# An audio block with routed experts on one core: later layer norm for the second half, roots by Newton steps, weights by quarters

## The chip, the core and the metric

One core of a Trainium2 chip runs the whole program. The core has five engines with queues of their own: TensorE (matmuls and transposes; PE), VectorE (DVE), ScalarE (ACT), GpSimd (POOL) and SyncE (SP, which issues transfers here). They wait for one another by semaphores. The metric is device time in microseconds, the median of several executions. Before the change it is 421.42 us (three runs, 420.96 to 422.04).

## The reference

The input x has 64 sequences of 125 steps with 128 features.

```
h   = QRNN(x)                 # window 3, tanh and sigmoid gates, scan over 123 steps
h   = h + gelu(longconv(LN(h)) + h0 * LN(h))
u   = LN(h)                   # layer norm over 128 features, the "second" one
p   = u @ gate.T              # 16 experts; top 2 of each token, softmax of the two as weights
s_e = sum over tokens that chose e of silu(u @ w1_e.T)
y_e = (s_e / count_e) @ w2_e.T
out = h + w_1 * y_(expert 1) + w_2 * y_(expert 2)
```

An expert gives one mean vector, so each token's u goes through w1 of its two experts, and only the sums are kept.

## The kernel before, in words

H holds h as 123 steps (partitions) x 64 sequences x 128. Up to 158 us the recurrent cell and the long convolution fill it. Then comes routing, in four quarters of 16 sequences, and then 138 expert tiles of 128 tokens.

The second layer norm has its statistics on VectorE (`bn`, one bn_stats per sequence, L1504; `moments2`, L1512 to L1520, makes variance `ve2`), its root on GpSimd (a power of -0.5, L594), `shift` on VectorE (L1525) and the rows themselves on ScalarE (`norm2`, L1186) and GpSimd (L597), 8 of 16 each in quarters 0 to 2 and all 16 on ScalarE in quarter 3. `write_table(g)` on SP (L504) stores a quarter of the normalized rows to a table in HBM, when both engines are done with it.

The router doesn't need normalized rows: `x2_transposes` (L714) and `logits` (L705) work on H, sixteen sets of four sequences, through a ring of two PSUM banks (`PR`) that ScalarE's `copy_x2T` (L1195) reads. The same ring takes the transposes of w1 (`w1_transposes` L697, `copy_w1T` L1123) and the products `matches` (L785), which ScalarE turns into one-hots (`low_onehots`, L1223). For each quarter VectorE does `top2` (L1554 to L1564, twelve dependent steps, with other work put between them by `between`), TensorE `ranks` (L738 to L757, waits for the mask), VectorE `counts` (L1568) and `places` (L1574 to L1591), TensorE `bit_transposes` (L777), ScalarE `copy_bits` (L1216), TensorE `matches` and `picks` (L768), ScalarE `copy_V` (L1210), TensorE `pick_transposes` (L793), VectorE `placed` (L1609, L1611). `codes` (L895) and `index_list` (L1693, L1695) then make a list of token rows by expert.

There are two lists. The first serves tiles 0 to 41, from quarters 0 and 1; the second the rest. `idx_ready` counts them. GpSimd then issues one indirect transfer (L614, a gather) for each tile, in order, from the table into a tile row. The first waits for list 1 and for quarters 0 and 1 of the table. Tile rows 0 to 59 are the rows of XN, in which the normalized sequences lay; so gather 32 waits until `write_table(2)` and `write_table(3)` have landed (`table_out[1]`), and gather 42 for list 2. `paces` holds a few more gathers behind steps of the routing:

```
paces = {8: (count_mm, 3), 12: (bits_mm, 3), 16: (pick_mm, 3), 20: (count_mm, 4), 23: (bits_mm, 4),
         27: (pick_mm, 4), 32: (code_mm, 2)}
```

A tile goes through TensorE (three transposes at a time, L905; one product with w1 of its expert, L935), ScalarE (silu, L1265) and VectorE (addition into `esum`, L1712). TensorE may be five tiles ahead of the additions. The first product waits for all of w1T; the first addition waits for four transfers that clear `esum`, each behind a set of w1 transposes (`clear`, L510, on SP's queue in the order written). Between the additions of tiles 15 to 18 VectorE makes the weights of the picks, all quarters at once (two products L1788, a sum L1790); TensorE transposes them at tiles 23 and 26 (`RT_AT`, L1025), ScalarE and VectorE split them in two parts (L1278, L1797). Behind the last tile come the means, w2 and the output.

On every engine instructions run in the order in which the code lists them, so a waiting instruction holds all that are behind it on that engine.

## Time and profile before

| what | us |
|---|---|
| median of the runs | 421.42 |
| the profiled execution | 420.74 |
| its span, first to last instruction | 419.0 |
| routing, from the last addition of the convolution to the first expert product | 158.6 to 234.6 |
| gathers, first to last issue | 199.74 to 373.66 |
| expert products and the last one's end | 234.56 to 381.97 |

Busy shares of the span are PE 91%, DVE 74%, ACT 52% and POOL 49%. A busy TensorE isn't TensorE at its peak, since pipelined matmuls are counted whole; what is read here is who waits for whom in each stretch. A row of a timeline gives start and duration in us, the engine, the line, the operation and, in brackets, how long the engine idled before it and what ended that. Rows that follow one another with the same form are merged (x16: sixteen). The granted clock (PEclk) is 1.00 at full speed, 2.4 GHz, and 0.50 at 1.2 GHz.

### The profile page before, as it was taken

The numbers are of one execution on the slowest core, as the hardware profiler recorded it, in microseconds if no ns is written. First come the engines' busy times: TensorE is split into PE (matmuls) and PEld (weight loads), VectorE is DVE, ScalarE is ACT, GpSimd is POOL, SyncE is SP. The second block draws the span as 40 slices with busy tenths as digits, with TensorE's granted clock in tenths as the row PEclk, the third lists the DMA queues.
The fourth block names the chain that finished last, engine by engine and source line by source line (L and its number), as shares of the span: only waits on it lengthen the run. The fifth ranks groups of instructions, "written<-read, shape, count | busy, mean of one in ns | idle before, by whom it ended". The sixth has DMA issues, their size and how long they took to land.

```text
span 419.0 us, 7310 instructions
## 1 busy us (share of the span) xinstructions
PE 379.5 (91%) x1929; PEld 261.9 (63%) x1930; DVE 310.8 (74%) x827; ACT 217.6 (52%) x423; POOL 206.0 (49%) x231
## 2 busy tenths in 40 slices
PE   7999999999978998977785998899999998999892
PEld 7888888888868998864553543444444443334471
DVE  3399887878796879999877278577777675557892
ACT  2433555555551334667747864576676664565310
POOL 2011211111164004999777777777777777752600
PEclk9999999999989999996866998999999999999997
DMA  6400843433132058330475621111771111110068
GB/s 163 133 2 13 218 132 89 128 91 96 48 98 77 22 158 245 99 96 2 145 243 195 209 59 44 50 52 56 257 251 53 50 56 50 53 49 0 1 162 225
DMA packets 53020, 43.68 MB, mean 104 GB/s; under 512 B 20686, under 2 KB 45980, under 8 KB 52732
## 3 DMA queue, kind: packets, MB, share of 16 engines
q1 hardware_dynamic: 44276, 32.09, 26.2%
q0 software_dynamic: 4416, 9.05, 7.3%
q10 hardware_dynamic: 4296, 2.15, 1.9%
q8 instruction: 15, 0.25, 0.3%
q14 instruction: 17, 0.14, 0.1%
HBM read 34.86 MB, written 8.42 MB: 103 GB/s over the span
## 4 chain that ended last, share of the span: by engine, by line
PE 55%; DVE 17%; POOL 16%; issue 6%; ACT 4%; DMA 1%; DVEq 0%; ACTq 0%; POOLq 0%
PE P L662 22%; PE P L935 11%; PE P L867 7%; POOL BIG L614 7%; POOL arena L614 5%; DVE H L1828 3%; DVE BIG L1712 3%; PE P L697 2%; PE P L1062 2%; PE P L655 2%; PE P L905 2%; PE P L688 2%; POOL XN L597 2%; DVE arena L1504 1%; POOL arena L594 1%
## 5 line engine op out<-in xcount | busy, mean ns | idle before, releaser
L935 PE MATMUL P<-w1T,arena 128*128 x276 | 129.0, 601 | 3.2 <-DVE BIG L1712 2.6
L1712 DVE TENSOR_TENSOR BIG<-BIG,P 128x512 f32 x138 | 94.9, 688 | 49.9 <-ACT P L1265 34.3
L935 PEld LDWEIGHTS P<-w1T,arena 128*128 128x128 f32 x276 | 48.5, 191 | 50.2 <-issue 49.5
L1265 ACT ACTIVATE P<-P 128x512 f32<-128x512 f32 x138 | 72.8, 580 | 1.6 <-PE P L935 1.5
L614 POOL DMA_INDIRECT XN<-table,arena x60 | 59.5, 991 | 19.1 <-issue 19.1
L557 POOL TENSOR_TENSOR rs<-ve,mhalf 123x4 f32<-123x4 f32 x16 | 17.5, 1096 | 101.8 <-DVE ve L1356 101.8
L1103 ACT ACTIVATE arena<-P 128x492 f32<-128x492 f32 x48 | 27.9, 583 | 50.3 <-PE P L662 50.3
L1254 ACT COPY arena<-P 128x384 f32<-128x384 f32 (+1 forms) x48 | 22.4, 467 | 53.4 <-PE P L935 53.3
L614 POOL DMA_INDIRECT arena<-table,arena x42 | 39.7, 944 | 12.8 <-issue 12.2
L662 PE MATMUL P<-xh,wh 128*128 128x498 f32 x144 | 42.4, 403 | 0.0
L662 PE MATMUL P<-xh,wl 128*128 128x498 f32 x144 | 40.5, 390 | 0.0
L662 PE MATMUL P<-xl,wh 128*128 128x498 f32 x144 | 40.4, 389 | 0.0
L614 POOL DMA_INDIRECT BIG<-table,arena x36 | 34.0, 944 | 11.0 <-issue 10.7
L662 PEld LDWEIGHTS P<-xl,wh 128*128 128x128 f32 x144 | 27.3, 190 | 5.6
L662 PEld LDWEIGHTS P<-xh,wl 128*128 128x128 f32 x144 | 27.1, 188 | 5.4
L867 PE MATMUL P<-XN,BIG 123*123 123x112 f32 (+1 forms) x256 | 27.7, 271 | 1.1 <-DVE XN L1401 1.1
L662 PEld LDWEIGHTS P<-xh,wh 128*128 128x128 f32 x144 | 26.2, 192 | 4.1
L867 PEld LDWEIGHTS P<-XN,BIG 123*123 123x123 f32 x256 | 27.6, 188 | 1.3 <-DVE XN L1401 1.3
L594 POOL TENSOR_TENSOR arena<-arena,mhalf 123x16 f32<-123x16 f32 x4 | 11.7, 2923 | 31.6 <-DVE arena L1520 31.6
L1359 DVE SCALAR_TENSOR_TENSOR arena<-arena 128x492 f32<-128x492 f32 x16 | 10.7, 669 | 17.2 <-ACT arena L1103 17.2
L597 POOL TENSOR_SCALAR XN<-H,arena 123x128 f32<-123x128 f32 x24 | 23.3, 985 | 0.3
L1499 DVE TENSOR_TENSOR H<-H,arena 123x512 f32<-123x512 f32 x16 | 20.2, 1279 | 3.7 <-ACT arena L1177 3.7
(242 smaller groups left out, 617.4 us busy)
## 6 DMA issues: line engine op xcount, KB each, us to landing
arena<-kpad SPq DMA_DIRECT2D x16, 492.0 KB, 4.0
XN<-in_L_ffn_w SPq DMA_DIRECT2D x1, 4096.0 KB, 17.0
arena<-in_x SPq DMA_DIRECT2D x16, 224.0 KB
table<-XN SPq DMA_DIRECT2D x4, 896.0 KB
BIG<-table SPq DMA_DIRECT2D x1, 2048.0 KB, 9.3
out<-H SPq DMA_DIRECT2D x8, 224.0 KB
out<-H ACTq DMA_DIRECT2D x8, 224.0 KB
BIG<-table SPq DMA_DIRECT2D x1, 1024.0 KB, 4.8
```

Of the source, the lines that this page charges most:

```text
L557: nc.gpsimd.tensor_tensor(rs1[0:T, k], ve1[0:T, k], mhalf[0:T, 0:CB], ALU.pow).then_inc(rstd1, 1)
L594: nc.gpsimd.tensor_tensor(rs2[0:T, qb], ve2[0:T, qb], mhalf[0:T], ALU.pow).then_inc(rstd2, 1)
L597: a = nc.gpsimd.tensor_scalar(XN[0:T, b], H[0:T, b], mm2[0:T, 0, b:b + 1], rs2[0:T, b:b + 1], ALU.subtract, ALU.mult)
L614: pool.indirect_dma_start(out=row_of(n), out_offset=None, in_=table[0:(QA * QB + 1) * TROW, :] if n < NA else table[:, :], in_offset=bass. ...
L662: mm = nc.tensor.matmul(PG[g][:, 0:NV], wpart[:, w, g * D:(g + 1) * D], xpart[:, k, w:w + NV], start=(place == 0 and w == 0), stop=(place ...
L867: mm = nc.tensor.matmul(PG[g % 3][0:T, j * B:j * B + n], hank[0:T, c // HP % HRES, c % HP], XF[0:T, c * B:c * B + n], start=True, stop=True)
L935: mm = nc.tensor.matmul(bank[:, :], stat, w1T[:, bass.ds(e * FF, FF)], start=True, stop=True)
L1103: nc.scalar.activation(dst[:, k].rearrange("p (b t) -> p b t", b=CB), src, func).then_inc(gate_act, 1)
L1254: nc.scalar.copy(GTs[:, bank, 0:count * SLOT], PT[:, 0:count * SLOT]).then_inc(GT_ready, 1)
L1265: nc.scalar.activation(bank[:, :], bank[:, :], ACT.Silu).then_inc(silu_done, 1)
L1499: v.tensor_tensor(hv, hv, gl[0:T, g % 2], ALU.add).then_inc(H_added, 1)
L1712: v.tensor_tensor(at, at, bank[:, :], ALU.add).then_inc(esum_step, 1)
```

## The change

- **The second half's layer norm** (quarters 2 and 3) moves behind the first list: its statistics, moments and shifts leave the places between the steps of top2(0) and top2(1) and go between and behind those of top2(2), top2(3) and the new steps.
- **The roots** of quarters 2 and 3 are made on VectorE by `rstd_by_steps`: an integer first guess and three Newton steps, eleven dependent operations on 123x16, with other work between them. GpSimd makes those of quarters 0 and 1 alone, both ahead of its norm rows.
- **The norm rows** of quarters 2 and 3 are all ScalarE's (`NORM_POOL`), at new places of its queue; four rows of quarter 1 go behind copy_V(0).
- **x2 and w1 sets**: thirteen sets of x2 come ahead of the first list, three behind it; no w1 set stands ahead of it (two did).
- **stay_warm**: matmuls of 256 or 512 columns into a bank that isn't read, on TensorE ahead of its waits in the routing.
- **The weights** of the picks are made by quarters, one operation of 256 columns behind each of the additions 14 to 25; the transposes come at tiles 23 and 32.
- clear(11, 0, 4) goes ahead of write_table(2) on SP.

The diff, without the lines around each place:

```diff
...
-NORM_POOL = (8, 8, 8, 0)
+NORM_POOL = (8, 8, 0, 0)
+X2_FIRST = 13
...
-        at_ring = 2 * NHB
-        for part, q in ((range(0, 2), 0), ((), 1), (range(2, 10), 2), (range(10, 12), 3)):
+        X2_AT = list(range(X2_FIRST))
+        at_ring = X2_FIRST
+        for part, q in (((), 0), ((), 1), (range(0, 10), 2), (range(10, 12), 3)):
+            if q == 2:
+                X2_AT += range(at_ring, at_ring + 2 * NHB - X2_FIRST)
+                at_ring += 2 * NHB - X2_FIRST
...
-        RT_AT = (23, 26)
+        R_AT = 14
+        RT_AT = (23, 32)
...
+            clear(11, 0, 4)
-            clear(11, 0, 4)
...
-            def norms(g):
+            def rstd_of(g):
+            def norms(g):
...
-            norms(0)
+            rstd_of(0)
+            rstd_of(1)
+            norms(0)
-            norms(2)
-            norms(3)
...
+            def stay_warm(n, wide=False):
+                place = P[1][:, :] if wide else P[3][:, 256:512]
+                cols = oneb[:].unsqueeze(1).to_broadcast([128, 4 if wide else 2, 128])
+                for _ in range(n):
+                    nc.tensor.matmul(place, oneb[:], cols, start=True, stop=True)
...
-                pe.wait_ge(ring_read, n + 1)
+                pe.wait_ge(ring_read, X2_AT[n] + 1)
...
-                if n >= 2:
-                    pe.wait_ge(ring_read, n - 1)
+                at = X2_AT[n]
+                if at >= 2:
+                    pe.wait_ge(ring_read, at - 1)
-                    mm = nc.tensor.transpose(PR[n % 2][:, q * T:(q + 1) * T], H[0:T, 4 * n + q], ident[0:T, 0:T])
+                    mm = nc.tensor.transpose(PR[at % 2][:, q * T:(q + 1) * T], H[0:T, 4 * n + q], ident[0:T, 0:T])
...
+                stay_warm((0, 4, 2, 1)[q], q >= 2)
...
+                    if n == ON_ACT - OG:
+                        stay_warm(3 if q < 2 else 1, q >= 2)
...
+                stay_warm((5, 6, 8, 4)[q], q >= 2)
+                stay_warm((4, 3, 1, 5)[q], q >= 2)
+                    if a == 2 and q == 0:
+                        tile_base(1)
+                    if a == 2 and q != 2:
+                        stay_warm(3 if q == 3 else 5, q == 3)
...
+                stay_warm(2 if q >= 2 else 4, q >= 2)
...
+                if nth == 2:
+                    stay_warm(4, True)
...
+                    if c >= chunks - 2:
+                        stay_warm((2 if c == chunks - 2 else 1) * (2 if nth == 1 else 1), nth == 2)
...
-            for n in range(2 * NHB):
+            for n in range(X2_FIRST):
-                if n == 11:
+                if n == 10:
-                if n == 15:
+                if n == 12:
-            logits(2 * NHB - 1)
+            logits(X2_FIRST - 1)
-            for m in range(0, 2):
-                w1_transposes(m)
-            tile_base(1)
...
-            for m in range(2, 8):
+            for n in range(X2_FIRST, 2 * NHB):
+                x2_transposes(n)
+                if n > X2_FIRST:
+                    logits(n - 1)
+            logits(2 * NHB - 1)
+            for m in range(0, 5):
-            for m in range(8, 10):
+            for m in range(5, 10):
...
-                    pe.wait_ge(R_ready, 1)
+                    pe.wait_ge(R_ready, 2 * (RT_AT.index(n) + 1))
...
-                act.wait_ge(ring_mm, n + 1)
+                act.wait_ge(ring_mm, X2_AT[n] + 1)
-                nc.scalar.copy(x2T[:, n % 2].rearrange("p b t -> p (b t)"), PR[n % 2][:, 0:4 * T]).then_inc(ring_read, 1)
+                nc.scalar.copy(x2T[:, n % 2].rearrange("p b t -> p (b t)"), PR[X2_AT[n] % 2][:, 0:4 * T]).then_inc(ring_read, 1)
...
-            for n in range(12, 16):
-                if n == 14:
-                    code_OH(0)
-                for b in NORM_ACT[1][2 * (n - 12):2 * (n - 11)]:
-                    norm2(b)
-                copy_x2T(n)
+            copy_x2T(12)
+            code_OH(0)
+            for b in NORM_ACT[1][:4]:
+                norm2(b)
-            for m in range(0, 2):
-                copy_w1T(m)
+            for b in NORM_ACT[1][4:]:
+                norm2(b)
-            for b in NORM_ACT[2]:
-                norm2(b)
-            for m in range(2, 8):
+            for n in range(X2_FIRST, 2 * NHB):
+                copy_x2T(n)
+            for m in range(0, 5):
...
-            for b in NORM_ACT[3][:6]:
+            code_OH(2)
+            for m in range(5, 10):
+                copy_w1T(m)
+            for b in NORM_ACT[2][:3]:
-            code_OH(2)
-            for m in range(8, 10):
-                copy_w1T(m)
+            for b in NORM_ACT[2][3:5]:
+                norm2(b)
+            code_OH(3)
+            for b in NORM_ACT[2][5:8]:
+                norm2(b)
-            code_OH(3)
+            for b in NORM_ACT[2][8:10]:
+                norm2(b)
-            for b in NORM_ACT[3][6:]:
+            for b in NORM_ACT[2][10:]:
+            for b in NORM_ACT[3]:
+                norm2(b)
...
-            shift(0)
...
-            top2(0, more_stats(2))
-            for b in range(2 * QB + (4 * 11 + 2) // 3, 3 * QB):
-                bn(b)
-            counts(0)
-            moments2(2)
-            shift(1)
+            def shifts(i):
+                if i in (2, 8):
+                    shift(i // 8)
+            top2(0, shifts)
+            def rstd_by_steps(g, between):
+                qb = slice(g * QB, (g + 1) * QB)
+                var, y = ve2[0:T, qb], rs2[0:T, qb]
+                square, half = mm2[0:T, 1, qb], mm2[0:T, 2, qb].bitcast(I32)
+                def then(ins, i):
+                    rs[0] += 1
+                    ins.then_inc(route_step, 1)
+                    between(i)
+                    dve.wait_ge(route_step, rs[0])
+                dve.wait_ge(ve2_ready, g + 1)
+                then(v.tensor_scalar(half, var.bitcast(I32), 1, None, ALU.arith_shift_right), 0)
+                then(v.tensor_scalar(y.bitcast(I32), half, -1.0, float(0x5F3759DF), ALU.mult, ALU.add), 1)
+                for k in range(3):
+                    then(v.tensor_tensor(square, y, y, ALU.mult), 3 * k + 2)
+                    then(v.scalar_tensor_tensor(out=square, in0=square, scalar=-0.5, in1=var, op0=ALU.mult,
+                                                op1=ALU.mult), 3 * k + 3)
+                    a = v.scalar_tensor_tensor(out=y, in0=square, scalar=1.5, in1=y, op0=ALU.add, op1=ALU.mult)
+                    if k == 2:
+                        a.then_inc(rstd2, 1)
+                    else:
+                        then(a, 3 * k + 4)
...
-            top2(1, more_stats(3))
-            for b in range(3 * QB + (4 * 11 + 2) // 3, 4 * QB):
-                bn(b)
+            def count_first(i):
+                if i == 2:
+                    counts(0)
+            top2(1, count_first)
-            moments2(3)
-            shift(2)
...
-            shift(3)
-            top2(2, nothing)
+            top2(2, more_stats(2))
+            for b in range(2 * QB + (4 * 11 + 2) // 3, 3 * QB):
+                bn(b)
+            moments2(2)
+            def stats_of_last(i):
+                bn(3 * QB + i)
+            rstd_by_steps(2, stats_of_last)
+            shift(2)
...
+            for b in range(3 * QB + 10, 4 * QB):
+                bn(b)
+            moments2(3)
-            placed(2)
-            low_onehots(3, 0)
+            def places_of_last(i):
+                if i == 2:
+                    placed(2)
+                if i == 5:
+                    low_onehots(3, 0)
+            rstd_by_steps(3, places_of_last)
+            shift(3)
...
-            for n in range(16):
+            def weight(k, q):
+                w = wgt[0:T, 1 + k, q * QB:(q + 1) * QB].unsqueeze(2).to_broadcast([T, QB, E])
+                rs[0] += 1
+                v.tensor_tensor((L, Ltmp)[k][0:T, q * QB:(q + 1) * QB], OH[0:T, q, k], w,
+                                ALU.mult).then_inc(route_step, 1)
+            def weights(n):
+                q, part = (n - R_AT) // 3, (n - R_AT) % 3
+                if part < 2:
+                    weight(part, q)
+                else:
+                    dve.wait_ge(route_step, rs[0])
+                    both = L[0:T, q * QB:(q + 1) * QB]
+                    v.tensor_tensor(both, both, Ltmp[0:T, q * QB:(q + 1) * QB], ALU.add).then_inc(R_ready, 1)
+            for n in range(R_AT):
-            by_quarter = [a[0:T].rearrange("p (q b) e -> p q b e", q=NQ) for a in (L, Ltmp)]
-            for k, dst in enumerate(by_quarter):
-                w = wgt[0:T, 1 + k].rearrange("p (q b) -> p q b", q=NQ).unsqueeze(3).to_broadcast([T, NQ, QB, E])
-                step(v.tensor_tensor(dst, OH[0:T, :, k], w, ALU.mult))
-                add_tile(16 + k)
-            v.tensor_tensor(L[0:T], L[0:T], Ltmp[0:T], ALU.add).then_inc(R_ready, 1)
-            for n in range(18, UNROLLED):
+            for n in range(R_AT, UNROLLED):
+                if n < R_AT + 3 * NQ:
+                    weights(n)
```

## Rows read from the trace of the kernel before

**Rows 1.** GpSimd's timeline (start us, us, engine, line, operation), first list to end

```profile
199.74 1.23 POOL L614 DMA_INDIRECT XN<-table,arena  x1 [1.17 <-issue]
...
240.74 0.94 POOL L614 DMA_INDIRECT XN<-table,arena  x1 [0.30 <-issue]
...
254.47 1.75 POOL L614 DMA_INDIRECT XN<-table,arena  x1 [0.30 <-issue]
...
259.02 1.94 POOL L614 DMA_INDIRECT XN<-table,arena  x1 [0.30 <-issue]
...
373.66 0.94 POOL L614 DMA_INDIRECT arena<-table,arena  x1 [0.30 <-issue]
```

**Rows 2.** TensorE's timeline, expert matmuls (L935)

```profile
234.56 2.84 PE L935 MATMUL P<-w1T,arena 128*128 x6 [0.17 <-issue]
...
267.97 2.74 PE L935 MATMUL P<-w1T,arena 128*128 x6
...
343.50 2.74 PE L935 MATMUL P<-w1T,arena 128*128 x6
...
375.78 1.02 PE L935 MATMUL P<-w1T,arena 128*128 x2
```

**Rows 3.** VectorE's timeline, ahead of the first list and the step behind it

```profile
167.12 0.41 DVE L1554 TENSOR_REDUCE arena<-P 123x16 f32<-123x256 f32 x1
...
173.51 0.27 DVE L1564 TENSOR_TENSOR BIG<-BIG 123x256 bf16<-123x256 bf16 x1
...
182.85 0.16 DVE L1568 CAST arena<-P 128x2 bf16<-128x2 f32 x1
...
183.80 0.68 DVE L1574 TENSOR_REDUCE arena<-P 123x32 f32<-123x512 f32 x1
...
198.63 0.25 DVE L1695 TENSOR_SCALAR arena<-arena,route_sb 128x42 int32<-128x42 int32 x1
...
199.04 0.40 DVE L1554 TENSOR_REDUCE arena<-P 123x16 f32<-123x256 f32 x1
```

**Rows 4.** VectorE's timeline, its idle times behind the first list

```profile
204.91 0.16 DVE L1568 CAST arena<-P 128x2 bf16<-128x2 f32 x1 [0.82 <-PE P L738]
...
215.16 0.16 DVE L1568 CAST arena<-P 128x2 bf16<-128x2 f32 x1 [1.11 <-PE P L738]
...
216.76 0.69 DVE L1574 TENSOR_REDUCE arena<-P 123x32 f32<-123x512 f32 x1 [1.30 <-PE P L749]
...
223.66 0.18 DVE L1765 TENSOR_SCALAR arena<-P 128x16 f32<-128x16 f32 x1 [2.78 <-PE P L879]
```

**Rows 5.** TensorE's timeline, transposes (L714) and 512-column matmuls (L729)

```profile
178.62 0.58 PE L714 MATMUL P<-ident,H 123*128 123x123 f32 x4
...
179.90 0.58 PE L714 MATMUL P<-ident,H 123*128 123x123 f32 x4
...
180.32 0.60 PE L729 MATMUL P<-samef,arena 128*123 128x512 bf16 x2
...
198.20 1.94 PE L729 MATMUL P<-samef,arena 128*123 128x512 bf16 x4
```

**Rows 6.** ScalarE's timeline, copy_bits, Relus and norm rows

```profile
191.21 0.26 ACT L1216 CAST arena<-P 128x123 bf16<-128x123 f32 x1 [0.22 <-PE P L777]
...
221.11 2.72 ACT L1223 ACTIVATE BIG<-P,below 123x512 bf16<-123x512 f32 x4 [0.57 <-PE P L785]
...
223.73 3.94 ACT L1186 ACTIVATE XN<-H,arena 123x128 f32<-123x128 f32 x10
```

**Rows 7.** DMA issues by size: median us from issue to landing

```profile
BIG<-table SPq DMA_DIRECT2D x1, 1024.0 KB, 4.8
...
BIG<-table SPq DMA_DIRECT2D x2, 512.0 KB, 6.1
```

**Rows 8.** VectorE's timeline, the sum of the weights

```profile
258.93 1.22 DVE L1790 TENSOR_TENSOR arena<-arena 123x1024 f32<-123x1024 f32 x1
```

**Rows 9.** stretches: us, busy (x) of PE, PEld, DVE, ACT, POOL, PEclk, DMA

```profile
192.00:194.00 2.00, 1.23 (x4) 0.35 (x2) 2.00 (x2) 1.56 (x3) 2.00 (x2) 0.50 0.00 0
```

## The prediction

> **What bounds the kernel now.** I read the chain of waits first, then the timelines of GpSimd, VectorE, TensorE and ScalarE from 158 us on. The chain gives the expert matmuls the stretch from 234 to 292 us and GpSimd's gathers the rest; the GpSimd timeline says more. Its 138 gathers run from 199.74 to 373.66 us [rows 1], all 1.25 us apart but for a few that last longer, and none of them idles more than the fixed 0.30 us ahead of it: the stream is one unbroken chain, and its start decides its end. The experts run at 75.53/26 = 2.905 us per three tiles between 267.97 and 343.50 us; at that pace tile 132 would start at 343.50 + 9 x 2.905 = 369.65 us, and it starts at 375.78 [rows 2]. So the expert stream has 6.1 us of slack, and the gathers bound the end. Everything behind the last gather is unchanged.
>
> The first gather follows the first list (VectorE's row at 198.63, done at 198.88 [rows 3]) by 0.86 us. VectorE is busy from 158 us to there almost without a gap, which is why work taken out of it ahead of the list should count.
>
> The profiled execution took 420.74 us, 0.68 us below the median of the runs, 421.42. The sum is made on the former and 0.68 added.
>
> **Ahead of the first list.** Thirty-two bn_stats, two moments2 and four shifts leave; two shifts return inside top2(0). top2(0) with its fill takes 167.12 to 173.51 and 0.27 for its last operation; a bare one takes 199.04 to 204.09 [rows 3, 4], 5.05. Without shift(0) it starts at 166.93, so the mask of quarter 0 is there at 166.93 + 5.05 = 172.0, that of quarter 1 near 177.0. The moments between counts(1), 182.85, and places(0), 183.80, go too: 0.87 us without the count's own 0.08, in four dependent levels, 0.22 a level [rows 3].
>
> TensorE is then late. shift(0) comes 1 us later, ScalarE's first norm2 and the copy behind it with it, and ranks(0) starts near 172.25, ends near 174.1. Up to ranks(1) stand two steps of transposes and logits (1.28 each, 178.62 to 179.90), one more set of logits (0.9), counts_behind (0.43 for two 512-column matmuls, 180.32 and what follows) and four 256-column fillers (0.43 by the same row): 4.35 us, so ranks(1) at 178.45 [rows 5]. counts(1) and places(0) follow at 178.8, against 183.80: 5.0 us gained there.
>
> It is not all kept. Five fillers stand ahead of bit_transposes(0) and end 0.55 us past the moment at which the bits are there, while the two w1 sets ahead of it are gone (0.4 us of ScalarE's copies): copy_V(0), which ended at 190.99 (0.22 of idle time ahead of 191.21 [rows 6]), ends 4.85 earlier, 186.15. ScalarE now has four norm rows (3.94/10 = 0.394 each, 1.6 us [rows 6]) between it and copy_bits(1), which so runs at 187.75, against 191.21. From there to the list it was 7.7 us, through matches, picks, copy_V(1), pick_transposes, placed(1) and codes; TensorE's part of it ran at half clock [rows 9], which I count 0.4 us shorter: **first list at 195.0, 3.9 us earlier**. Bounds: 2.8 (no clock gained, the fillers in full) and 5.0 (VectorE's own path). The wait for ScalarE's rows holds only this chain; VectorE, which would be ready for placed(1) 1 us sooner, stands idle. The table's first half, written once ScalarE's last row of quarter 1 is done (187.75), is down before that.
>
> Were nothing else late, the gathers would start and end 3.9 us earlier.
>
> **Behind the first list.** A gather has to wait there. Gather 32 overwrites row 32, which write_table(3) reads, and so waits for table_out[1]. Before, gather 32 ran at 240.74 [rows 1] with that write long down: the last norm row ended at 227.67 (223.73 + 3.94 [rows 6]). The same gather would now want to run at 236.85. I follow when ScalarE ends its last row now.
>
> VectorE: from the first list to total_mm(2) took 198.88 to 223.66, 24.8 us, of which 0.82, 1.11, 1.30 and 2.78 us are idle [rows 4]. Added: 15 bn_stats inside top2(2) and one behind (6.39 + 0.27 against 5.05, and 0.2: 1.9), moments2(2) 0.9, rstd_by_steps(2) with ten bn_stats (0.1 + 0.2 each, and a last one: 3.2 with its shift), six bn_stats 1.2, moments2(3) 0.9, rstd_by_steps(3) 2.3 (eleven levels of 0.22, less what placed(2) and low_onehots(3, 0) cover, plus its shift): 10.4 us. The idle time takes 4.9 of it: ranks(2) is ready near 203.1 (counts_behind, three sets of x2 and logits, 4.2 us with their copies, five w1 sets at the 0.6 us of a copy, two wide fillers, from 194.3 on), which leaves 0.4 idle, and total_mm(2) leaves 0.7. So this point moves from 223.66 to 195.0 + 24.8 + 5.5 = 225.3: the 3.9 us are spent and 1.6 more.
>
> TensorE and ScalarE: places(3) starts at 195.0 + 17.9 (198.88 to 216.76) + 8.1 added - 2.8 absorbed = 218.2. ranks(3) ends near 218.4; pick_transposes(2) 0.9, two w1 sets 1.0 and four wide fillers 0.85 (0.21 each) put bit_transposes(3) at 221.15, behind its bits; copy_bits to 221.7; two norm rows to 222.5; the four Relus of quarter 3's matches, started at 222.9, 2.6 us as before [rows 6], to 225.5; six rows of quarter 2, 2.4, to 227.9, by when picks(3) are done; copy_V(3) 0.35; and then all sixteen rows of quarter 3, 6.3 us, which stand behind copy_V(3) in the queue and need shift(3) besides (near 224.5): **last row at 234.55, 6.9 us later than before**.
>
> write_table(3) then needs, by the nearest rows, 4.8 us (1 MB) to 6.1 us (512 KB) from issue to landing [rows 7]; I take 5.2, near the one of its size. With 0.1 to issue and 0.4 to wake GpSimd, **gather 32 runs at 240.25**, 3.4 us after it would have and 0.5 us before its old time. The other paces (count_mm, bits_mm, pick_mm, code_mm) come at most 0.3 us from binding and earlier than this one; code_mm(2), near 238.3, is inside it.
>
> **Behind that.** Three 1.22 us operations of VectorE made the weights. Beside two of them a gather took 1.75 and 1.94 us in place of 0.94, 1.8 us in all; the one at 259.02 began just after VectorE's at 258.93 and ended 0.9 us after it [rows 1, 8]. Now twelve of about 0.33 us stand there. A gather that meets one at a random point waits half of it: 12 x (0.33/1.25) x 0.17 = 0.5 us. Gain 1.3 us; bounds 1.8 (none met) and -1.5 (ten gathers, each met for a whole one, 3.3).
> The Trainium skill, "SBUF — State Buffer", section "SBUF: two separate sides", says that a VectorE operation with two SBUF inputs and a GpSimd operation that reads SBUF exclude each other for the whole instruction. The rows agree on the blocking. By that rule, with a loss that goes with the locked time (12 x 0.33 = 4.0 us against 3.7), nothing would be regained here.
>
> The expert stream: w1T is complete behind ScalarE's last norm row and four copies, so tile 0 starts near 238.2 (234.56 before [rows 2]). The last clears of esum now queue on SP behind write_table(3); with 6.1 us each [rows 7] VectorE's first addition, and with it tile 6, comes some 4.4 us later. Against its pace from tile 0 the stream lost 267.97 - (234.56 + 9 x 2.905) = 7.3 us up to tile 27, mostly to the weights; now at most VectorE's twelve added operations stand there, 4.0 us. So it moves by 4.4 - 7.3 + 4.0 = 1.1 us at the worst and has 6.1 of slack: it stays hidden, and costs one for one past 4.3 us (6.1 less the gathers' gain).
>
> **Sum.** -0.5 (gather 32) - 1.3 (gathers less blocked) = -1.8: 420.74 - 1.8 + 0.68 = **419.6 us**.
>
> **Rivals.**
> 1. Full gain: ScalarE's last row ends by 230.7, no wait at gather 32, -3.9 - 1.3: 416.2. For it: ScalarE idles often behind 199 us, and TensorE's lower clock in the old second half may give back more than I took. Against it: sixteen rows in one piece. 14%.
> 2. No change: the first list gains only the lower bound, 2.8, everything behind shifts by 1.1 and half of the blocking gain fails (0.6): -0.1, 421.3. Here belongs the case by the rule above: -0.5 alone, 420.9. 25%.
> 3. Slower: the fillers keep no clock and stand on the path. Before, the clock was 0.50 of full speed (1.2 GHz) at 192 to 194 us while TensorE was idle for four tenths of the time [rows 9], and four 512-column matmuls took 1.94 us at 198.20 against 0.60 for two at 180.32 [rows 5]. At that level the wide ones cost 0.49 each; the four ahead of bit_transposes(3), the five ahead of matches(3) and slower w1 sets put the Relus 4.2 us later, and with them the last row, the write and gather 32: +3.7 - 1.3 = +2.4, 423.8. It is slower than before from 1.8 us of such delay on. For it: the chip falls to that level in these very gaps. Against it: the fillers close them. 14%.
> My forecast holds the rest, 47%, with 418.2 to 420.9 as its own range (landing 4.8 to 6.1, blocking 0 to 2).
>
> Faster or slower counts from 0.3% (1.26 us), about what a measurement of this kernel can tell. Faster: rival 1 and four fifths of the forecast, 0.53; slower: rival 3 and a little, 0.15; the same: 0.32. The range 416.3 to 423.0 leaves out some of rivals 1 and 3, 18% together.
>
> **What would show it.** Right: first gather near 195.9 us; a gap of 2 to 5 us on GpSimd ahead of gather 32, released by a DMA; ScalarE's last norm row near 234.5; no gather above 1.3 us beside the weights; no idle time on TensorE at tiles 23 to 32. Wrong: no gap at gather 32 (rival 1), a first gather behind 197 us, a clock near 0.5 behind the first list (rival 3), or tiles behind 120 that never wait for a gather (the expert stream then bounds).

## The result, and the profile after

The changed kernel takes 419.42 us (median of 7, 418.02 to 419.67) beside 421.58 (420.79 to 422.74) for the kernel before: ratio 0.9941, 95% interval 0.9922 to 0.9960, a gain of 0.6%. Over all 26 of its runs here it lies between 417.27 and 420.08. Its profiled execution took 419.67 us with a span of 417.9. That is 1.07 below the profile of before, while the medians stand 2.16 apart: the old profile lies 0.84 below 421.58, and the new one 0.25 above its own median.

GpSimd's timeline answers to [rows 1]: the first and the last gather, those that something other than issue held, and those over 1.0 us beside the weights.

```profile
194.81 1.23 POOL L622 DMA_INDIRECT XN<-table,arena  x1 [9.52 <-DVE arena L1756]
...
211.60 0.94 POOL L622 DMA_INDIRECT XN<-table,arena  x1 [1.69 <-PE P L797]
...
217.86 0.94 POOL L622 DMA_INDIRECT XN<-table,arena  x1 [0.79 <-PE P L787]
...
241.44 0.94 POOL L622 DMA_INDIRECT XN<-table,arena  x1 [3.36 <-DMA table<-XN]
...
260.15 1.09 POOL L622 DMA_INDIRECT XN<-table,arena  x1 [0.30 <-issue]
...
264.04 1.15 POOL L622 DMA_INDIRECT XN<-table,arena  x1 [0.30 <-issue]
...
269.24 1.16 POOL L622 DMA_INDIRECT XN<-table,arena  x1 [0.30 <-issue]
...
373.08 0.94 POOL L622 DMA_INDIRECT arena<-table,arena  x1 [0.30 <-issue]
```

The stream starts 4.93 us earlier than in [rows 1] and is broken at gather 32, which waits for the table's write: 241.44 in place of 240.74. So the lead of 4.93 is a lag of 0.70 there. Of these 5.63 us the wait takes 3.06 (3.36 less the 0.30 that stands ahead of every gather), the paces at gathers 12 and 16 take 1.39 and 0.49, and 0.7 goes to gathers that last longer than before. From gather 32 on the gathers take 131.64 us in place of 132.92, and the last is 0.58 ahead of the old one.

VectorE's timeline, for [rows 3 and 4]: the convolution's last addition, counts(1) (which waits for TensorE's ranks(1)), places(0), the first list's last operation, and the one that waits for total_mm(2).

```profile
157.47 1.24 DVE L1537 TENSOR_TENSOR H<-H,arena 123x512 f32<-123x512 f32 x1 [0.45 <-ACT arena L1209]
...
178.87 0.16 DVE L1606 CAST arena<-P 128x2 bf16<-128x2 f32 x1 [1.59 <-PE P L755]
178.94 0.68 DVE L1612 TENSOR_REDUCE arena<-P 123x32 f32<-123x512 f32 x1
...
194.26 0.25 DVE L1756 TENSOR_SCALAR arena<-arena,route_sb 128x42 int32<-128x42 int32 x1
...
226.26 0.18 DVE L1844 TENSOR_SCALAR arena<-P 128x16 f32<-128x16 f32 x1 [0.37 <-PE P L905]
```

ScalarE's timeline, for [rows 6]: the four norm rows, copy_bits(1), quarter 3's Relus, six rows of quarter 2, and all sixteen of quarter 3.

```profile
186.15 1.65 ACT L1218 ACTIVATE XN<-H,arena 123x128 f32<-123x128 f32 x4
187.70 0.25 ACT L1248 CAST arena<-P 128x123 bf16<-128x123 f32 x1
...
224.00 2.47 ACT L1255 ACTIVATE BIG<-P,below 123x512 bf16<-123x512 f32 x4 [0.46 <-PE P L810]
226.36 2.40 ACT L1218 ACTIVATE XN<-H,arena 123x128 f32<-123x128 f32 x6
228.84 0.37 ACT L1242 COPY arena<-P 128x256 f32<-128x256 f32 x1
229.11 6.27 ACT L1218 ACTIVATE XN<-H,arena 123x128 f32<-123x128 f32 x16
```

The last row ends at 229.11 + 6.27 = 235.38, and gather 32 runs 6.06 us later.

TensorE, for [rows 2]: ranks(1), a w1 set behind ScalarE's rows, tile 6, the first transposes of the weights, the row that stood at 343.50, the first wait for a gather, and tile 132.

```profile
178.63 0.19 PE L755 MATMUL P<-oneb,BIG 123*128 123x1 bf16 x2
...
235.99 1.94 PE L712 MATMUL P<-ident,BIG 128*128 128x128 f32 x8 [5.01 <-ACT w1T L1155]
...
247.48 2.90 PE L965 MATMUL P<-w1T,arena 128*128 x6 [0.77 <-DVE BIG L1773]
...
265.47 0.64 PE L1057 MATMUL P<-ident,arena 123*128 123x123 f32 x4 [0.57 <-DVE arena L1874]
...
345.56 2.74 PE L965 MATMUL P<-w1T,arena 128*128 x6
...
360.70 0.54 PE L935 MATMUL P<-ident,BIG 128*128 128x128 f32 x3 [0.56 <-DMA BIG<-table,arena]
...
375.20 1.02 PE L965 MATMUL P<-w1T,arena 128*128 x2
```

Its stretches, for [rows 9] (PEclk is the number behind POOL's):

```profile
192.00:194.00 2.00, 1.75 (x18) 1.06 (x18) 1.12 (x4) 0.06 (x1) 0.00 (x0) 1.00 0.26 69
...
212.00:220.00 8.00, 7.79 (x61) 3.80 (x60) 6.32 (x23) 5.55 (x11) 5.99 (x6) 0.57 0.32 114
```

The clock is full (2.4 GHz) at 192 to 194 us, where it had been half. In 212 to 220 it falls towards 1.2 GHz, as it did before the change (0.58 there), behind 1.35 us in which TensorE idled (209.65 to 211.01) for quarter 2's bits. That idle time alone isn't the reason: weights_whole, below, has the same 1.35 us there and a clock of 1.00 behind it.

### The profile page after: what moved, and what is told of

Its sections match the earlier page's. It is cut to its first block, busy times and chain, and to the rows that moved or that the text cites. A ratio compares the mean times of both kernels' runs of the same rounds, so it can differ in the third digit from the quotient of the medians.

```text
span 417.9 us, 7515 instructions
## 1 busy us (share of the span) xinstructions
PE 386.5 (92%) x2018; PEld 266.3 (64%) x2019; DVE 314.8 (75%) x858; ACT 220.5 (53%) x431; POOL 191.6 (46%) x221
## 4 chain that ended last, share of the span: by engine, by line
PE 67%; DVE 18%; ACT 6%; issue 3%; DMA 2%; POOL 1%; DVEq 1%; SPq 0%; ACTq 0%; POOLq 0%
PE P L965 23%; PE P L670 19%; PE P L893 7%; PE P L935 3%; DVE H L1919 3%; DVE BIG L1773 2%; DVE arena L1542 2%; ACT XN L1218 2%; DMA BIG<-table 2%; PE P L1094 2%; PE P L663 2%; PE P L695 2%; PE P L720 2%; PE P L703 1%; DVE arena L1403 1%
## 5 line engine op out<-in xcount | busy, mean ns | idle before, releaser
L965 PE MATMUL P<-w1T,arena 128*128 x276 | 127.4, 596 | 1.4 <-DVE BIG L1773 1.0
L1209 ACT ACTIVATE arena<-P 123x512 f32<-123x512 f32 x16 | 9.6, 598 | 21.9 <-PE P L893 20.5
L600 POOL TENSOR_TENSOR arena<-arena,mhalf 123x16 f32<-123x16 f32 x2 | 5.8, 2914 | 32.3 <-DVE arena L1558 32.3
```

Of the source, the lines that this page charges most:

```text
L965: mm = nc.tensor.matmul(bank[:, :], stat, w1T[:, bass.ds(e * FF, FF)], start=True, stop=True)
```

## The experiments

Ratios are to the kernel before on the same chip (medians 421.19, 422.17 and 421.01 in the three groups). A "profile" of an experiment is one execution.

**after_again, after_third**: the changed kernel itself, beside the first and the third group.

> The changed kernel once more, for the spread and a second trace. Theory (the gather stream bounds the end; gather 32 waits for write_table(3)): the first gather near 194.8 us, gather 32 at 240.5 to 242 behind a wait of about 3 us, the time 0.9922 to 0.996 of before. Rival (the gain of the median comes from somewhere the first trace does not show): gather 32 or the last gather at another place than 241.4 and 373.1 by over 1 us.

> The changed kernel once more, beside the three kernels below. 419.0 to 419.7 us, ratio 0.993 to 0.996; gather 32 waits 3 to 3.5 us for the table's write where the clock falls in 212 to 220 us, 1 to 1.5 us where it doesn't (as in weights_whole, whose program is the same up to there).

419.33 us (12 runs), 0.9946 (0.9929 to 0.9964), and 419.47 (7 runs), 0.9947 (0.9926 to 0.9967). Gather 32 waits 3.44 and 3.32 us in their profiles and runs at 241.35 and 241.21; the clock is 0.57 in 212 to 220 in both. The effect of the change is there each time.

**gate_split**: gather 32 waits for quarter 2's rows alone.

```
table_out: 2 semaphores -> 3, g // QA -> max(g - 1, 0)
before gather 32: - wait table_out[1] for both quarters   + for quarter 2's
before gather 42: + wait table_out[2] (quarter 3)
paces: - 32: (code_mm, 2)
```

> Gather 32 waits for write_table(2) alone (its rows are of quarter 2), gather 42 for write_table(3); code_mm(2) no longer holds gather 32. Theory: no wait at gather 32, it runs at 238.4 instead of 241.4 us, every later gather 3.0 us earlier; the expert stream has 354.28 + 6 x 2.905 = 371.7 against 375.2 us, 3.5 us of slack, so the time falls by 2.5 to 3.1 us below the changed kernel, to about 416.4 us. Rival (the expert stream, which starts 6.2 us later than before, bounds the end by now): gather 32 earlier all the same, the time within 1 us of the changed kernel.

417.94 us, 0.9929 (0.9903 to 0.9954): 1.4 us by the medians, half of what was expected, and the interval overlaps after_again's. The trace says it more clearly: the wait is gone from its GpSimd timeline, though in its profile the first gather came at 195.54:

```profile
195.54 1.23 POOL L622 DMA_INDIRECT XN<-table,arena  x1 [10.79 <-DVE arena L1757]
...
239.58 0.94 POOL L622 DMA_INDIRECT XN<-table,arena  x1 [0.30 <-issue]
...
370.74 0.94 POOL L622 DMA_INDIRECT arena<-table,arena  x1 [0.30 <-issue]
```

The gate (the one wait that holds the whole stream) did hold the gathers: the last of them is 2.34 us earlier than in the changed kernel, and from the first to the last they take 175.20 us in place of 178.27. The expert stream then waits for a gather once only, 0.24 us at 369.63: it is then close to bounding the end itself.

**half_rows**: eight of quarter 3's sixteen rows are not normalized. **half_both**: besides, five of the last six rows of quarter 2.

```
- for b in NORM_ACT[3]:           + for b in NORM_ACT[3][8:]:
- for b in NORM_ACT[2][10:]:      + for b in NORM_ACT[2][15:]:     (half_both)
```

> Left out: the normalizing of eight of the sixteen rows of quarter 3. ScalarE's last row ends 3.15 us earlier, and w1T and the first expert tile come as much earlier. Theory: gather 32 again at 238.4 us (it would run there without a wait), the time 2.7 to 3.3 us below the changed kernel, as with the wait split. Rival (the expert stream bounds): here it starts earlier too, so this one gains and the split wait does not.

> half_rows, and of the last six rows of quarter 2 all but one left out too (thirteen rows of the 32 in the second half are not normalized). Theory (half_rows gained only 1.0 us at gather 32 because the write of quarter 2's rows is issued behind their last one, at 228.7 us, and the last quarter's write queues behind it in the DMA queue): quarter 2's write is issued 1.5 to 2 us earlier, gather 32 runs before 238.7 us in place of 240.37, with a wait below 1 us, and the time is 1 to 1.7 us below half_rows', near 417.3 us. Rival (the clears of esum that share the DMA engines set the landing): gather 32 stays near 240, the time within 0.4 us of half_rows'.

half_rows: 418.82 us, 0.9943 (0.9923 to 0.9963). The expectation failed: the last row ends 3.2 us earlier, gather 32 runs 1.07 earlier. The DMA view of 228 to 246 us shows where the rest went (40 slices, busy tenths of the 16 DMA engines). First the changed kernel:

```profile
DMA  0222999999998714005899999999958999956206
```

and half_rows:

```profile
DMA  0405999999989999999999689969996753402204
```

In the changed kernel quarter 2's write is done before quarter 3's begins (the slices near zero). In half_rows the second follows on the first's heels, the engines have no gap for some twelve microseconds, and gather 32 waits to 240.37. Of the 3.2 us that ScalarE gave back 2.1 were lost there: from the last row to gather 32 it is 8.20 us in place of 6.06.

half_both: 418.46 us, 0.9933 (0.9913 to 0.9953), where near 417.3 was expected. Quarter 2's write is issued at 226.51 in place of 228.65 and gather 32 doesn't wait, but its profile's first gather came at 196.29, so it ran at 240.33 for that reason. The time lies 0.4 us below half_rows', on another chip. Whether quarter 2's write or the clears of esum, which share the DMA engines, held half_rows' gather isn't told apart.

**no_fill**: no stay_warm matmuls.

> The changed kernel without any filler matmul. Theory (the fillers hold the clock and cost a little in the path): the clock falls to 0.5 from about 188 us to the end of the first list; the first list 0 to 0.8 us later, ScalarE's last norm row and gather 32 0 to 1 us later, time +0 to +1.2 us against the changed kernel. Rival (the fillers are only in the way): first list 0.5 us earlier, last norm row 0.5 to 1.5 us earlier, time 0.5 to 1.5 us lower.

420.35 us (420.09 to 421.03, 11 runs), 0.9982 (0.9968 to 0.9996): 1.0 us above the changed kernel beside it, clear of its interval. So the fillers make 1.0 of the 1.9 us by which the changed kernel is faster there. The clock by stretches, and the steps to the first gather and gather 32:

```profile
184.00:192.00 8.00, 5.19 (x63) 3.10 (x60) 6.87 (x26) 4.97 (x11) 0.43 (x1) 0.50 0.47 126
...
212.00:220.00 8.00, 7.76 (x57) 3.68 (x58) 6.64 (x24) 5.44 (x12) 5.71 (x6) 0.50 0.34 120
```

```profile
156.97 1.24 DVE L1537 TENSOR_TENSOR H<-H,arena 123x512 f32<-123x512 f32 x1 [0.45 <-ACT arena L1209]
...
186.33 0.25 ACT L1248 CAST arena<-P 128x123 bf16<-128x123 f32 x1
...
193.73 0.25 DVE L1756 TENSOR_SCALAR arena<-arena,route_sb 128x42 int32<-128x42 int32 x1
...
194.28 1.23 POOL L622 DMA_INDIRECT XN<-table,arena  x1 [9.85 <-DVE arena L1756]
...
241.88 0.94 POOL L622 DMA_INDIRECT XN<-table,arena  x1 [3.55 <-DMA table<-XN]
```

Its first gather comes half a microsecond ahead of the changed kernel's, but that lead stands at the convolution's last addition already (156.97 for 157.47), ahead of the first filler; from there to the first gather the two take the same time. The fillers put copy_bits(1) 1.37 us later (187.70 for 186.33), 0.87 more than that lead, and the full clock gives it back: from there to the end of the list it is 6.81 us with them and 7.65 without. Behind the list they gain: without them gather 32 runs 0.44 us later, 0.94 counted from the last addition.

**fill_more**: fourteen fillers in place of eight ahead of bit_transposes(2).

```
- stay_warm((5, 6, 8, 4)[q], q >= 2)     + stay_warm((5, 6, 14, 4)[q], q >= 2)
```

> The changed kernel with fourteen in place of eight filler matmuls ahead of the transposes of quarter 2's bits, so that TensorE is not idle from 209.65 to 211.01 us, ahead of the stretch 212 to 220 us in which the granted clock falls to about 0.57. Theory (the fall of the clock there makes the second half 1 to 2 us later in most executions and not in some, which is why the changed kernel's times spread over 417.3 to 420.0 us): clock 1.00 in 212 to 220, ScalarE's last row near 234.4 in place of 235.4, gather 32 near 240.4, the time 418.3 to 418.8 us with a smaller spread. Rival (that stretch waits for VectorE's bits and places, not for TensorE): clock up, last row and time unchanged, 419.2 to 419.6 us.

418.18 us (417.31 to 418.56, 5 runs), 0.9909 (0.9884 to 0.9934). The stretch and the gathers:

```profile
212.00:220.00 8.00, 7.20 (x75) 4.41 (x74) 7.74 (x33) 6.20 (x13) 6.17 (x7) 1.00 0.33 110
```

```profile
194.83 1.23 POOL L622 DMA_INDIRECT XN<-table,arena  x1 [9.49 <-DVE arena L1756]
...
239.65 0.95 POOL L622 DMA_INDIRECT XN<-table,arena  x1 [1.05 <-DMA table<-XN]
...
371.13 0.95 POOL L622 DMA_INDIRECT arena<-table,arena  x1 [0.30 <-issue]
```

The six fillers fill 1.3 us of idle time. The clock stays full and gather 32 runs 1.79 us earlier than in the changed kernel, more than expected. That the fillers did it isn't shown: the next run, on the same chip, has the clock at 1.00 and gather 32 at 239.50 without them, and the changed kernel itself didn't run there. The ratio is 0.0037 lower than after_again's, from another chip, and the intervals overlap by a sliver.

**weights_whole**: the weights as before the change.

```
- weight(part, q) behind additions 14 to 25   + three whole operations behind additions 15 to 17
RT_AT: (23, 32) -> (23, 26)
```

> The changed kernel with the picks' weights made as before the change: three whole operations of VectorE behind additions 15 to 17, both transposes behind tiles 23 and 26; all else as changed. Theory (twelve short operations block the gathers less than three long ones, 0.58 against 1.8 us, and the expert stream, which has only 3.5 us of slack left, then loses some 4 us more at tiles 23 to 27 than now): last gather near 374.3 in place of 373.1, two gathers of 1.7 to 1.9 us, and the end 1.2 to 2.0 us later than the changed kernel's, 420.6 to 421.3 us beside its 419.4. Rival (the rule by which the loss goes with the locked time, 4.0 against 3.7 us): no later than the changed kernel, 419.0 to 419.7 us.

419.76 us (418.78 to 422.35, 9 runs), 0.9957 (0.9930 to 0.9983), where 420.6 to 421.3 was expected: the time is not told apart from the changed kernel's. The clock, TensorE's idle time ahead of that stretch and the gathers are:

```profile
212.00:220.00 8.00, 7.20 (x74) 4.38 (x75) 7.71 (x33) 6.40 (x13) 6.17 (x7) 1.00 0.30 101
```

```profile
210.85 0.32 PE L797 MATMUL P<-ident,arena 123*128 123x123 f32 x1 [1.35 <-DVE arena L1626]
```

```profile
239.50 0.94 POOL L622 DMA_INDIRECT XN<-table,arena  x1 [1.12 <-DMA table<-XN]
...
259.47 1.99 POOL L622 DMA_INDIRECT XN<-table,arena  x1 [0.30 <-issue]
...
264.26 1.94 POOL L622 DMA_INDIRECT XN<-table,arena  x1 [0.30 <-issue]
...
372.64 0.94 POOL L622 DMA_INDIRECT arena<-table,arena  x1 [0.30 <-issue]
```

From gather 32 to the last they take 133.14 us, 1.50 more than the changed kernel's 131.64, as the first theory has it. In this execution the clock was 1.00 in 212 to 220 with the code up to there unchanged, gather 32 ran at 239.50, and the loss doesn't show in its time; whether it was so in the other eight isn't known.

**paces_off, split_w1first, split_w1first_nopace, best**: the six paces at gathers 8 to 27 (in paces_off all seven) taken out; w1's last four copies ahead of ScalarE's sixteen rows and the last clears ahead of the last write, with gate_split; both; and both with fill_more's fillers.

```
paces_off, ..._nopace, best:  paces = {}
split_w1first, ..._nopace, best:  gate_split, and
+ for m in range(12, E): copy_w1T(m)      (moved ahead of NORM_ACT[3])
+ clear(13, 4, 6); clear(15, 6, 8)        (moved ahead of write_table(3))
best: fill_more's line too
```

> The changed kernel without the seven paces of GpSimd's gathers 8 to 32, its wait for the table's write kept. Theory (gather 32's wait for the write sets the second half, and covers the 1.88 us that the paces take at gathers 12 and 16): gather 31 ends 1.9 us earlier, gather 32 waits 1.9 us longer and runs when it did, and the time is within 0.4 us of the changed kernel's. Rival (the paces keep gathers from blocking VectorE, as their places suggest: without them VectorE's steps come later and the write with them): gather 32 0.5 us or more later, 0.5 to 1 us slower. Second rival (the paces cost 1.9 us whatever waits behind): 1 us or more faster.

> The table's write in three semaphores as in gate_split, and besides ScalarE's copies of the last four w1 sets ahead of its sixteen rows of quarter 3, and the last two clears of esum ahead of the last part of the table on SP. Theory (with gather 32 free, the expert stream is within a microsecond of the end, since its w1 sets stand behind the sixteen rows and its first addition behind the clears): tile 0 starts 4 to 5 us earlier than in gate_split, the expert stream never bounds, no wait for w1 sets at half clock; the time is gate_split's or up to 0.5 us below, 417.3 to 418.0 us, and tile 132 regains 3 us or more of slack. Rival (the quarter's rows come 1.5 us later and gather 42 then waits for them, or the clears and the write share the DMA engines): 0.5 to 1.5 us slower than gate_split.

> split_w1first without the six paces that make GpSimd wait, at gathers 8 to 27, for TensorE's signals. Theory (the paces cost what the idle times at gathers 12 and 16 show, 1.39 + 0.49 = 1.9 us in the changed kernel, and nothing takes their place while the expert stream has slack): gathers end 1 to 1.9 us earlier than in split_w1first, 415.5 to 417.0 us. Rival (without the paces the gathers block VectorE's steps of the second half or are blocked by them, or the last rows' write then holds gather 42): within 0.4 us of split_w1first.

> split_w1first_nopace with fill_more's fourteen fillers. Theory (both together: the gathers are an unbroken chain from the first list on, so the fillers' gain in the second half now lies off the path): within 0.5 us of split_w1first_nopace, 415.4 to 416.4 us, 3 to 4 us below the changed kernel beside it, with nothing left on GpSimd but gathers that last longer beside VectorE. Rival (a clock that falls in 212 to 220 us in some executions delays the index list of the second half, code_mm and the last rows enough to hold gather 32 or 42): 0.5 to 1 us faster still by its median, and a smaller spread.

paces_off: 418.67 us (417.38 to 419.98), 0.9941 (0.9920 to 0.9963), beside 419.47, 0.9947: no difference that can be measured. Gather 32 still waits for the table's write, so its wait covers the paces:

```profile
240.36 0.94 POOL L622 DMA_INDIRECT XN<-table,arena  x1 [2.36 <-DMA table<-XN]
```

The wait didn't grow by 1.9 us, as the theory had it, but is 1.0 shorter. The clock was 1.00 in 212 to 220 in that profile, and the write came 1.1 us earlier; the gathers up to 31 last 1.4 us longer in sum than in the changed kernel's profile (1.0 longer in gate_split's too, which has the paces and the same clock there).

split_w1first: 418.30, 0.9911 (0.9885 to 0.9937), within gate_split's interval. Tile 0 was expected 4 to 5 us earlier than in gate_split, where it starts at 239.79; it comes at 239.45. TensorE waits 4.52 us there for ScalarE's copy of the tile's transposes, which stands behind the sixteen rows too:

```profile
238.65 0.52 PE L936 MATMUL P<-ident,XN 128*128 128x128 f32 x3 [4.52 <-ACT arena L1285]
...
239.45 4.32 PE L966 MATMUL P<-w1T,arena 128*128 x6 [0.29 <-issue]
```

split_w1first_nopace: 415.87 (415.62 to 418.41), 0.9861 (0.9833 to 0.9889), 2.4 us below split_w1first by the medians of five runs each, with intervals that overlap by a sliver. Its profiled execution is the slowest of the five, with the first gather at 197.22:

```profile
197.22 1.23 POOL L622 DMA_INDIRECT XN<-table,arena  x1 [11.12 <-DVE arena L1756]
...
240.13 0.95 POOL L622 DMA_INDIRECT XN<-table,arena  x1 [0.30 <-issue]
```

With the gate gone the paces are on the path. From the first gather to gather 32 it is 42.91 us here and 42.78 in best, against 44.03 in split_w1first and 44.04 in gate_split: 1.1 to 1.3 us, most of the 1.39 that gather 12 waits in those two.

best: 416.26 (415.62 to 417.52), 0.9892 (0.9872 to 0.9912), 3.2 us below the changed kernel beside it; over split_w1first_nopace the six fillers add nothing that can be measured. Its gathers:

```profile
194.72 1.23 POOL L622 DMA_INDIRECT XN<-table,arena  x1 [9.51 <-DVE arena L1756]
...
237.50 0.94 POOL L622 DMA_INDIRECT XN<-table,arena  x1 [0.30 <-issue]
...
368.88 0.94 POOL L622 DMA_INDIRECT arena<-table,arena  x1 [0.30 <-issue]
```

No gather waits, and TensorE doesn't wait for one either between 340 us and the end. Both last versions beat both kernels.

## Why the prediction was right

Step by step:

- **First list, predicted 3.9 us earlier.** The chain runs as written: ranks(1) at 178.63 (178.45), copy_bits(1) at 187.70 (187.75). The list is done at 194.51, 4.37 earlier; GpSimd's wake (from the list to the first gather) took 0.30 in place of 0.86, so the first gather gains 4.93. The 0.4 us credited to the clock were 0.84: 6.81 us from copy_bits(1) to the list, and 7.65 in no_fill at half clock. The fillers ahead of copy_bits(1) cost as much. The 1.0 us by which the first gather beat its forecast is worth nothing in the time, since gather 32 waits.
- **Gather 32, predicted 0.5 us earlier, is 0.70 later.** This is the mis-sized term, by 1.2 us. The place and the releaser are as forecast (a gap of 2 to 5 us released by a DMA: 3.36), and gate_split shows that it held the stream. One reason given for it is wrong: row 32 is the first of quarter 2, so write_table(2) reads it; the gather waits for write_table(3) only because the two writes share one semaphore, which is why splitting it was possible. ScalarE's last row ends at 235.38 for 234.55, as quarter 3's Relus start at 224.00 for 222.9. Ahead of them the clock is 0.57: the part of rival 3 that came true, and a sign of being wrong that the prediction had named. Two errors partly cancel here: in weights_whole, the same program up to there with the clock at 1.00, the Relus start at 221.99 and gather 32 runs at 239.50. The working was 0.9 too late for a full clock, and the fall of the clock, which its sum left out, goes with 2.0 the other way. The other 0.36 is the landing with its issue and wake, 6.06 for 5.7; no row gave the 0.1 and the 0.4 in that term.
- **Paces, "at most 0.3 us from binding".** Wrong in size: 1.39 and 0.49 us at gathers 12 and 16. Harmless, as paces_off shows, since gather 32 waits anyway. But it makes the agreement of the gap (3.36 measured, 3.4 forecast) luck: gather 32 could have run at 238.38, not 236.85, and ran 1.2 us later than forecast.
- **Weights, predicted 1.3 us.** [rows 1, 8] against the rows above: 132.92 - 131.64 = 1.28. The loss is 0.15 + 0.21 + 0.22 = 0.58, expected 0.5, though each operation took 0.42 us, not 0.33. So close a match is partly luck: with the same twelve operations the loss is 0.05 in gate_split's profile and 0.19 in paces_off's. The rule of the Trainium skill ("SBUF — State Buffer", section "SBUF: two separate sides"), that a VectorE operation with two SBUF inputs and a GpSimd operation that reads SBUF exclude each other for the whole instruction, agrees with the long gathers (1.99 and 1.94 us). That the loss goes with the locked time was my own addition, and it failed: the locked time grew from 3.7 to 12 x 0.42 = 5.0 us and the loss fell from 1.8 to 0.58; weights_whole brings two gathers of 1.99 and 1.94 back.
- **Expert stream, predicted at most 1.1 us later and hidden.** It is 2.06 later (345.56 against 343.50), so that bound was too low: tile 0, expected at 238.2, starts at 240.74. It waits for the w1 sets behind the sixteen rows, with the clock at 0.51 in 233 to 240, and for ScalarE's copy behind them (split_w1first). TensorE idles 0.57 us at tile 23, where none was forecast. Its slack fell from 6.1 us to 375.20 - (345.56 + 9 x 2.905) = 3.5 us (360.70 is its first wait for a gather), and it stayed hidden.
- **Sum.** -1.8 was predicted; the two profiles differ by 1.07 (+0.70 - 1.28, and 0.5 behind the last gather: 419.0 - 373.66 = 45.34 against 417.9 - 373.08 = 44.82, which in the other profiles lies at 44.5 to 45.2 with the same code). That the forecast of 419.6 lies 0.2 us from the median of 419.42 is partly luck: the medians differ by more (2.16) than these two executions do, and beside the other two groups by 1.86 and 1.54. Small slips in the working (4.35 us where the terms make 4.32, a gather that ended 0.81 and not 0.9 us after VectorE's operation, 0.53 where the chances make 0.52) change nothing.

**What stays open** is why the executions differ. The code up to the first list is the same in all the profiles but no_fill's, yet:

| profiles | first gather | PEclk 184 to 200 | PEclk 212 to 220 |
|---|---|---|---|
| changed kernel (3), half_rows | 194.7 to 194.8 | 1.00 | 0.57 |
| weights_whole, fill_more, best | 194.7 to 194.8 | 1.00 | 1.00 |
| gate_split, split_w1first, paces_off, half_both | 195.3 to 196.3 | 0.89 | 1.00 |
| split_w1first_nopace | 197.22 | 0.79 | 1.00 |

Where the clock falls ahead of the list, the first gather is up to 2.5 us later (0.7 of it, in split_w1first_nopace, stands at the convolution's end already); where it doesn't fall there, it may fall behind. Without the six fillers it fell there in four of five such profiles, with them in neither of two, which is too few to show that they hold it. The changed kernel's times spread over 2.8 us, against 0.9 for no_fill, whose clock was low in both stretches. That the clock causes the spread is argued, not shown: the kernel before, at 0.73 and 0.58, spreads over 2.8 us too (29 runs beside after_again).

## What to carry to other kernels

Work moved behind a point gives its gain back at the next gate that waits for all of it: list the gates of the stream that bounds, and see whether one semaphore holds it for more than the first use needs (gate_split). A pace or a stall upstream of such a gate costs nothing until the gate is opened, and then most of it; open the gate first, then measure the rest. Before crediting a gain to an edit, look how far apart the two traces are ahead of the edit (no_fill's lead), and whether a run without it shows the same (fill_more and weights_whole). One long operation that blocks a stream may be worth cutting up even if the pieces are longer in sum.

## What the runs showed of the hardware

A quarter's write of 984 KB (896 and 88) let gather 32 run 6.06 us after ScalarE's last row, and 8.20 us after it where another such write had been issued 3.5 us ahead (half_rows). The Trainium skill ("Trainium Kernel Development and Optimization", section "Key Constraints") says that DMAs from all the issuing engines share the same 16 DMA engines. The trace agrees: in half_rows, from 229 to 237 us, SP's queue takes 84.6% of their time and the gathers' queue 9.6%. And code that is the same up to there can meet different clocks from one execution to the next: 1.00, 0.89 and 0.79 in 184 to 200 us, with the first gather at 194.7 to 197.2.
